# Self-loop products of two node groups in one step, their edge sums in the next; two PSUM banks for the sums and four for the products

## What is computed

```python
h = relu(layernorm(x))
W_rel = einsum('rb,bdf->rdf', w_comp, weight)          # 32 matrices out of 8 bases
agg = segment_sum(h[src] * norm, etype * n_nodes + dst) # edges sorted by dst
node = einsum('rnd,rdf->nf', agg, W_rel) + h_bias + h @ loop_weight
out = x + relu(node)
```

## Time and profile before

| | |
|---|---|
| median of three runs | 1015.2 us |
| the profiled execution | 1015.24 us |
| its span, first to last instruction | 1013.5 us (so 1.7 us lie around it) |
| TensorE busy | 990.3 us, 98% |
| VectorE busy | 955.0 us, 94% |
| ScalarE busy | 884.6 us, 87% |
| GpSimd busy | 723.8 us, 71% |
| granted TensorE clock | 0.999 |

### The profile page before, as it was taken

How to read it: one execution, slowest core, us unless ns; L and a number is a source line. 1 busy time by engine, 2 the same in 40 slices (tenths; PEclk the granted TensorE clock), 3 DMA queues, 4 the chain that set the end, 5 groups by cost and what they waited for, 6 DMA issues and landing times.

```text
span 1013.5 us, 23775 instructions
## 1 busy us (share of the span) xinstructions
PE 990.3 (98%) x4902; PEld 574.4 (57%) x4902; DVE 955.0 (94%) x4366; ACT 884.6 (87%) x3242; POOL 723.8 (71%) x1282
## 2 busy tenths in 40 slices
PE   5899999999999999999999999999999999999996
PEld 2355555555556565656565555555555655555655
DVE  6999999999999999999999999999999999999995
ACT  6898989898888889898989898989898988889884
POOL 6877777777777777777777777777777777777740
PEclk9999999999999999999999999999999999999999
DMA  4556555556556555565565555465655655555544
GB/s 116 145 135 165 149 156 164 156 144 169 143 152 173 140 154 161 152 166 155 143 173 141 154 162 158 138 178 140 168 152 152 166 148 155 159 155 141 156 123 140
DMA packets 178223, 154.47 MB, mean 152 GB/s; under 512 B 17781, under 2 KB 151213, under 8 KB 178077
## 3 DMA queue, kind: packets, MB, share of 16 engines
q1 hardware_dynamic: 157261, 101.40, 35.6%
q0 software_dynamic: 20384, 51.32, 19.7%
q10 hardware_dynamic: 432, 0.22, 0.1%
HBM read 101.31 MB, written 51.56 MB: 151 GB/s over the span
## 4 chain that ended last, share of the span: by engine, by line
PE 93%; DVE 2%; POOL 2%; issue 1%; ACT 1%; DMA 1%; DVEq 0%; ACTq 0%; POOLq 0%
PE y_ps L790 33%; PE y_ps L797 31%; PE win_ps L812 9%; PE win_ps L807 8%; PE hT_ps L876 4%; PE hT_ps L803 4%; PE mix_ps L868 1%; POOL xg L578 1%; DVE sum_a L1019 1%; DVE sum_b L1019 0%; DMA xg<-x,idx 0%; DVE msg L1052 0%; PE y_ps L812 0%; DMA src_all<-src 0%; PE y_ps L807 0%
## 5 line engine op out<-in xcount | busy, mean ns | idle before, releaser
L578 POOL DMA_INDIRECT xg<-x,idx x392 | 382.0, 974 | 73.4 <-issue 34.0
L790 PE MATMUL y_ps<-w_all,hT 128*128 128x512 f32 x784 | 412.3, 608 | 2.9 <-DVE sum_a L1019 2.7
L797 PE MATMUL y_ps<-w_all,hT 128*128 128x512 f32 x784 | 400.3, 592 | 0.0
L523 POOL TENSOR_TENSOR u<-z 128x128 f32<-128x128 f32 x392 | 180.4, 460 | 182.8 <-ACT z L626 178.9
L626 ACT ACTIVATE z<-y_ps,mix 128x128 f32<-128x128 f32 x784 | 244.5, 366 | 44.8 <-PE y_ps L797 37.8
L1019 DVE SCALAR_TENSOR_TENSOR sum_b<-y_ps,mix,sum_b 128x128 f32<-128x128 f32 x784 | 265.8, 339 | 0.0
L797 PEld LDWEIGHTS y_ps<-w_all,hT 128*128 128x128 f32 x784 | 149.1, 190 | 187.9 <-issue 164.0
L790 PEld LDWEIGHTS y_ps<-w_all,hT 128*128 128x128 f32 x784 | 132.3, 189 | 119.1 <-DVE sum_a L1019 60.9
L622 ACT ACTIVATE z<-y_ps,mix 128x128 f32<-128x128 f32 x392 | 140.8, 359 | 63.6 <-issue 44.9
L660 ACT ACTIVATE hw<-xw,shift,nrstd 128x128 f32<-128x128 f32 x391 | 192.6, 494 | 0.4 <-DVE shift L1121 0.4
L1019 DVE SCALAR_TENSOR_TENSOR sum_b<-y_ps,mix,z 128x128 f32<-128x128 f32 x392 | 131.4, 335 | 36.1 <-issue 32.3
(11 more groups left out here) (107 smaller groups left out, 1174.3 us busy)
## 6 DMA issues: line engine op xcount, KB each, us to landing
seg<-msgs SPq DMA_DIRECT2D x391, 104.8 KB
msgs<-msg SPq DMA_DIRECT2D x98, 258.0 KB
xw<-x POOLq DMA_DIRECT2D x97, 256.0 KB
out<-res SPq DMA_DIRECT2D x97, 256.0 KB
xg<-x,idx POOLq DMA_INDIRECT x392
type_bc<-type_rows SPq DMA_DIRECT2D x52, 112.0 KB
w_all<-weight SPq DMA_DIRECT2D x1, 512.0 KB
type_bc<-type_rows SPq DMA_DIRECT2D x4, 80.0 KB
```

The costliest lines, as they stand in the source:

```text
L523: nc.gpsimd.tensor_tensor(u[:, r, :], z[:, r, 0, :], z[:, r, 1, :], ALU.add).then_inc(s_u, 1)
L578: nc.gpsimd.indirect_dma_start(xg[:, q, j, :], None, x, bass.IndirectOffsetOnAxis(ap=idx[:, q, j:j + 1], axis=0)).then_inc(s_gather[q * G ...
L790: nc.tensor.matmul(y_ps[2 * t % 5][:, :, :], hT[:, q, j, :], w_all[:, B // 2:B, :], start=True, stop=True).then_inc(s_y_high, 1)
L797: nc.tensor.matmul(y_ps[(2 * t + 1) % 5][:, :, :], hT[:, q, j, :], w_all[:, 0:B // 2, :], start=True, stop=True).then_inc(s_y, 1)
```

## The change

- The five banks `y_ps` become four, and `win_ps` becomes two banks, used by even and odd node groups. Tile t now has its high product in bank 2t mod 4 and its low product in bank (2t+1) mod 4, so product_high waits for `s_b` of tile t-2 and product_low for `s_a` of tile t-2.
- TensorE does no self-loop products and edge sums in every step. In odd steps g it does the self-loop products of node groups g-7 and g-6 (8 matmuls), in even steps g the edge sums of node groups g-8 and g-7 (16 matmuls), with two node groups open in the two banks in between.
- `pick` moves one step later (VectorE step k+6). `res` of both groups of a pair is made in the even step: the first between slots 1 and 2 behind `pick`, the second behind slot 3, ahead of `hotT`.
- `hwT` and `pick` have three buffers in place of two; a new semaphore `n_self` counts the self-loop products and frees `hwT`.
- There is one more step at the end. The last four node groups use the four `y_ps` banks.

The diff, cut to its core:

```diff
+TRING = 3
+SELF_AT = 7
+PICK_AT = 8
+ROWS_AT = 6
-    STEPS = NGW + SUMS_AT
+    STEPS = NGW + PICK_AT - 1
-        hwT = sb("hwT", [P, HRING, G, P])
+        hwT = sb("hwT", [P, TRING, G, P])
-        pick = sb("pick", [P, HRING, G, HALVES, HALF])
+        pick = sb("pick", [P, TRING, G, HALVES, HALF])
-        y_ps = [psum(f"y_ps{b}", [P, B // 2, F]) for b in range(5)]
-        win_ps = psum("win_ps", [P, G, F])
+        y_ps = [psum(f"y_ps{b}", [P, B // 2, F]) for b in range(4)]
+        win_ps = [psum(f"win_ps{b}", [P, G, F]) for b in range(2)]
...
         def win_of(k):
-            return win_ps if k < NGW - LATE else late_bank(k - (NGW - LATE))
+            return win_ps[k % 2] if k < NGW - LATE else y_ps[k - (NGW - LATE)]
...
             def window_hT(k):
                 act.wait_ge(n_hT, k + 1)
-                if k >= HRING:
-                    act.wait_ge(n_y, k - (HRING - 1))
+                if k >= TRING:
+                    act.wait_ge(n_self, k - (TRING - 1))
...
             def product_high(g, q, j):
                 t = g * G + j
-                if t >= 3:
-                    pe.wait_ge(s_a, 2 * (t - 2))
+                if t >= 2:
+                    pe.wait_ge(s_b, 3 * (t - 1))
...
             def product_low(g, q, j):
                 t = g * G + j
                 if t >= 2:
-                    pe.wait_ge(s_b, 3 * (t - 1))
+                    pe.wait_ge(s_a, 2 * (t - 1))
...
             def window_self(k, j):
...
-                    elif k > 0:
-                        pe.wait_ge(n_res, k)
+                    if k >= NGW - LATE:
+                        pe.wait_ge(s_b, 3 * NG * G)
+                        pe.wait_ge(s_a, 2 * NG * G)
+                    elif k > 1:
+                        pe.wait_ge(n_res, k - 1)
...
-                if node_group(g, SUMS_AT) is not None:
-                    for j in range(G):
-                        window_self(g - SUMS_AT, j)
-                if node_group(g, SUMS_AT) is not None and g != STEPS - 2:
-                    if g == STEPS - 1:
-                        window_sums(NGW - 2)
-                    window_sums(g - SUMS_AT)
+                k = node_group(g, SELF_AT)
+                if k is not None and k % 2 == 0:
+                    for j in range(2 * G):
+                        window_self(k + j // G, j % G)
+                k = node_group(g, PICK_AT)
+                if k is not None and k % 2 == 0:
+                    window_sums(k)
+                    window_sums(k + 1)
...
-                if g == STEPS - 3:
-                    window_results(g - SUMS_AT)
-                if node_group(g, TURN_AT) is not None:
-                    window_rows(g - TURN_AT)
-                if node_group(g, SUMS_AT) is not None and g != STEPS - 3:
-                    window_results(g - SUMS_AT)
+                k = node_group(g, PICK_AT)
+                ready = k is not None and k % 2 == 0
+                late = ready and k >= NGW - LATE
+                if late:
+                    window_results(k)
+                    window_results(k + 1)
+                if node_group(g, ROWS_AT) is not None:
+                    window_rows(g - ROWS_AT)
+                if ready and not late:
+                    window_results(k)
                 tile_slot(g, n, q, 2, False)
...
                 tile_slot(g, n, q, 3, False)
                 stats_of(3)
+                if ready and not late:
+                    window_results(k + 1)
```

More of the change, by code:

```diff
@@ L245, in product @@
             high = base >= B // 2
-            return y_ps[(2 * t + (0 if high else 1)) % 5][:, base % (B // 2), :]
-        def late_bank(i):
-            return y_ps[(2 * NG * G + i) % 5]
+            return y_ps[(2 * t + (0 if high else 1)) % 4][:, base % (B // 2), :]
         def win_of(k):
-            return win_ps if k < NGW - LATE else late_bank(k - (NGW - LATE))
+            return win_ps[k % 2] if k < NGW - LATE else y_ps[k - (NGW - LATE)]
         s_iotas = sem("s_iotas")
@@ L355, in build_layer @@
         n_y = sem("n_y")
+        n_self = sem("n_self")
         n_res = sem("n_res")
@@ L419, in load_node_constants @@
                 sp.dma_start(pick[SEG_P:SEG_P + 1, :, :, :, :].rearrange("p r j c n -> p (r j) (c n)"),
-                             ones[SEG_P:SEG_P + 1, :].unsqueeze(1).to_broadcast([1, HRING * G, P])).then_inc(s_loop, 16)
+                             ones[SEG_P:SEG_P + 1, :].unsqueeze(1).to_broadcast([1, TRING * G, P])).then_inc(s_loop, 16)
                 sp.wait_ge(s_front, 1)
@@ L666, in window_hT @@
                 act.wait_ge(n_hT, k + 1)
-                if k >= HRING:
-                    act.wait_ge(n_y, k - (HRING - 1))
-                nc.scalar.activation(hwT[:, k % HRING, :, :], hT_ps[:, :, :], ACT.Copy).then_inc(n_hT_sb, 1)
+                if k >= TRING:
+                    act.wait_ge(n_self, k - (TRING - 1))
+                nc.scalar.activation(hwT[:, k % TRING, :, :], hT_ps[:, :, :], ACT.Copy).then_inc(n_hT_sb, 1)
             def step(g, n, q):
@@ L774, in count_bins @@
             def count_bins(half):
-                counts = win_ps[0:1, :, :].rearrange("p b f -> p (b f)")
+                counts = win_ps[0][0:1, :, :].rearrange("p b f -> p (b f)")
                 pe.wait_ge(s_first_hot, 1)
@@ L787, in product_high @@
                 t = g * G + j
-                if t >= 3:
-                    pe.wait_ge(s_a, 2 * (t - 2))
-                nc.tensor.matmul(y_ps[2 * t % 5][:, :, :], hT[:, q, j, :], w_all[:, B // 2:B, :],
+                if t >= 2:
+                    pe.wait_ge(s_b, 3 * (t - 1))
+                nc.tensor.matmul(y_ps[2 * t % 4][:, :, :], hT[:, q, j, :], w_all[:, B // 2:B, :],
                                  start=True, stop=True).then_inc(s_y_high, 1)
@@ L795, in product_low @@
                 if t >= 2:
-                    pe.wait_ge(s_b, 3 * (t - 1))
-                nc.tensor.matmul(y_ps[(2 * t + 1) % 5][:, :, :], hT[:, q, j, :], w_all[:, 0:B // 2, :],
+                    pe.wait_ge(s_a, 2 * (t - 1))
+                nc.tensor.matmul(y_ps[(2 * t + 1) % 4][:, :, :], hT[:, q, j, :], w_all[:, 0:B // 2, :],
                                  start=True, stop=True).then_inc(s_y, 1)
@@ L806, in self_loop @@
             def self_loop(bank, v, j):
-                nc.tensor.matmul(bank[:, j, :], hwT[:, v, j, :], w_loop[:, :], start=j == 0, stop=False)
+                return nc.tensor.matmul(bank[:, j, :], hwT[:, v, j, :], w_loop[:, :], start=j == 0, stop=False)
             def edge_sums(bank, v, q, windows):
@@ L822, in window_self @@
                     pe.wait_ge(n_hT_sb, k + 1)
[L823 to L829, removed]
-                    elif k > 0:
-                        pe.wait_ge(n_res, k)
+                    if k >= NGW - LATE:
[3 more added lines that the diff above has]
+                        pe.wait_ge(n_res, k - 1)
                 if j < windows_of(k):
-                    self_loop(win_of(k), k % HRING, j)
+                    mm = self_loop(win_of(k), k % TRING, j)
+                    if j == windows_of(k) - 1:
+                        mm.then_inc(n_self, 1)
             def window_sums(k):
                 pe.wait_ge(n_pick, k + 1)
-                edge_sums(win_of(k), k % HRING, k % SRING, windows_of(k)).then_inc(n_y, 1)
+                edge_sums(win_of(k), k % TRING, k % SRING, windows_of(k)).then_inc(n_y, 1)
             def step(g, n, q):
@@ L905, in _ @@
                     for j in range(G):
-                        self_loop(win_ps, 0, j)
-                    edge_sums(win_ps, 0, 0, G).then_inc(f_y, 1)
+                        self_loop(win_ps[0], 0, j)
+                    edge_sums(win_ps[0], 0, 0, G).then_inc(f_y, 1)
         @block.vector
@@ L963, in row_table @@
                 dve.wait_ge(s_hist, 1)
-                nc.vector.tensor_copy(hist[:, :], win_ps[0:1, :, :].rearrange("p b f -> p (b f)")[:, 0:BINS]).then_inc(s_meta, 1)
+                nc.vector.tensor_copy(hist[:, :], win_ps[0][0:1, :, :].rearrange("p b f -> p (b f)")[:, 0:BINS]).then_inc(s_meta, 1)
                 dve.wait_ge(s_meta, 1)
@@ L1132, in window_rows @@
             def window_rows(k):
-                if k >= HRING:
-                    dve.wait_ge(n_y, k - (HRING - 1))
+                if k >= TRING:
+                    dve.wait_ge(n_y, k - (TRING - 1))
                 dve.wait_ge(n_rel, k + 1)
-                one_hot_rows(k % HRING, k % NRING, windows_of(k)).then_inc(n_pick, 1)
+                one_hot_rows(k % TRING, k % NRING, windows_of(k)).then_inc(n_pick, 1)
             def results(bank, r, q, windows):
@@ L1248, in again @@
                 hold(dve, passed["dve"])
-                results(win_ps, 0, 0, G).then_inc(f_res, 1)
+                results(win_ps[0], 0, 0, G).then_inc(f_res, 1)
             with dve.If(compact > 0):
```

## The result

| | before | after |
|---|---|---|
| median | 1015.55 us (4 runs) | 1153.61 us (4 runs) |
| ratio | | 1.136, 95% interval 1.134 to 1.137 |
| span of the profiled execution | 1013.5 us | 1151.4 us |
| TensorE busy | 990.3 us, 98% | 1025.7 us, 89% |
| VectorE busy | 955.0 us, 94% | 981.1 us, 85% |

The forecast was 1142 us with a range of 1115 to 1170. The kernel became 138 us slower, 11.6 us more than forecast.

What follows compares the result with a forecast made beforehand. TensorE, 98% of the span, was taken to bound the kernel. With bank waits making a longer loop, span 1013.5 + 123.4 + 1.2 + 1.9 = 1140, and 1.7 around it, gave 1142 us; range 1115 to 1170.

Steps and rivals of the forecast that it cites:

- The bank releases: TensorE's low products: with four banks, `sum_a` frees the bank 0.59 us late for low m0, 1.10 for low m1.
- Slot 3 hangs on T: VectorE starts slot 3 at T+2.51 whatever TensorE does, because it waits for ScalarE's `z`, which follows T.
- T: Start of the edge transposes on TensorE in a step, from which the prediction counts its times.
- The second res in the loop at 0.60: VectorE, between slots 3 and 0: the second `res` makes `sum_a` of m3 0.60 us later in every other loop.
- The saving of 0.33 us per round trip: TensorE entering (0.14) and leaving (0.19) half-width sums once per two steps: about 46 x 0.33 = 15 us saved.
- the tail: End of the run: last edge step +1.2 us, sums of groups 94 and 95 behind the last transposes +1.9.
- Restart of 0.10: TensorE product behind a bank wait: the wait costs 0.10 us extra, bounds 0 and 0.19.
- the fourth rival: TensorE's clock falls because it idles; one loop in ten at 1.2 GHz adds 90 us, giving 1232; 2%.
- GpSimd and seg, taken at nothing: Later `res` delays SyncE's `seg` loads, holding GpSimd half a microsecond; covered by a microsecond, so no cost taken.
- the faster rival: Product banks are free in time and the regrouping's saving stands: 1002 us; 5%.
- The sum over steps 7 to 97: 45 pairs of loops, 11.27 and 11.53 us, 22.80 per pair in place of 20.07: 1026.0 us.
- The start: First steps, up to the loop of step 6: change of 0 us, give or take 2.

Runs made afterwards that it cites:

- the control: Kernel before, five banks and no regrouping, with the mix product moved into the transposes' bank behind messages(3) and VectorE's mix behind slot 3: 1022.3 us, ratio 1.0065.

## Why the prediction was right

- **The bank releases.** Right as read. The two waits, the instruction that ends them and the loop through ScalarE and VectorE are in the trace, to within 0.1 us; the four banks alone cost 125.6 us. One sign was mis-sized: I had said some 137 us of TensorE idle, 3.1 per pair, and the trace has 0.49 + 0.83 + 0.49 + 0.23 = 2.04 per pair, 103.5 in all. I counted from the time at which the product was due. The record of the product ahead reaches 0.16 us beyond that (1.02 against 0.86), and the restart of 0.10 falls behind the start.
- **Slot 3 hangs on T.** Right: T+2.51 in both loops shown; only with the block moved ahead of it did it come later, at T+2.79. This is what made the sum possible; had VectorE followed TensorE's delay in another way, the rows of before would not have told the new step.
- **The second res in the loop at 0.60.** Right: 27.5 us for 45.
- **The saving of 0.33 us per round trip.** The sum holds: 13.0 us against the control with five banks, where the forecast terms give 46 x 0.33 less 2 for the tail, 13. In the changed kernel it lies inside the loop and so is taken off it: 15.0 us between the two kernels with four banks. The measured parts, 125.6 for the banks, 15.0 off for the regrouping and 27.5 for the second `res`, lead from the kernel before to the changed one step by step and make its 138.
- **Restart of 0.10.** Right: a product behind a wait is followed after 0.96 (604.70 to 605.66), others after 0.86. By the 166 ns that the Trainium skill ("TensorE: Matmul & The Clock Gate", Single matmul latency) has for an isolated bf16 matmul the run would be 6 us longer, as an estimate. The loops, 11.56 and 11.27 against 11.53 and 11.27 with the row, decide for the row here. That the run is 6.4 us longer over steps 7 to 97 has other reasons, named below.
- **The clock.** TensorE idled in every loop and the granted clock was 1.00 of the 2.4 GHz level from 72 to 1115 us and up to the last matmul, so the fourth rival did not come. The run with five banks and later stores shows such a fall, on an idle time longer than any in the loops. In the tail of its profiled execution TensorE waited 2.51 us for `pick`, and the 28 matmuls behind that took 2.96 us in place of the 1.75 shown above:

```profile
1001.78 2.96 PE L813 MATMUL y_ps<-seg,pick 105*64 105x128 f32 x28 [2.51 <-DVE pick L1128]
```

The granted clock was 1.00 up to 1002 us and 0.52 from 1002 to 1005, near the 1.2 GHz level. That execution took 1011.03 us, the other four 1008.7 to 1009.3.
- **GpSimd and seg, taken at nothing.** The cost was right, the size of the wait was not. I had half a microsecond and some covered waits; in steps 6 to 97 there were 36 of 1.0 us in the mean. In the loop shown above SyncE issues the loads, and GpSimd takes them, like this:

```profile
601.60 1.89 SPq L442 DMA_DIRECT2D seg<-msgs  x4
```

```profile
606.39 0.20 POOL L548 TENSOR_TENSOR rel<-seg,half_off 104x8 f32<-104x8 f32 x1 [0.96 <-DMA seg<-msgs]
```

`res` ends 0.6 us before T and not 0.8; the first load is issued 1.2 us behind that, where my sum has 0.5 to 1; and so `rel` starts at T+5.39 and not at T+4.5 to T+5. The waits cost nothing in these steps because the bank waits covered them. Without these they cost 36 us, so in the faster rival the 1002 us could not have come either.
- **Mis-sized terms, 11 us together.** The sum over steps 7 to 97 came out 6.4 us short. I had listed what stands behind slot 3 and left out the nine order checks at its end, which the loop then carried: 3.8 us measured; some 1.4 us are the 0.03 us per pair by which the loops are longer; the last 1.2 us, in a few single loops, I have not taken apart. The start cost 2.9 and not 0, since the bank waits were there before any node work. The tail was 2 us longer than its term, by two waits for `pick` behind the last seg loads; with later stores they are gone, and the tail is 3.3 us longer than before, where I had 3.1.

## What to carry to other kernels

Where an engine is busy without a gap, the order behind it may still depend on slack that no busy share shows: write down for each buffer when it is wanted and when it is released, and move the want by what the change moves it. If the release is late, look for what the releasing instruction itself waits on; if that leads back to the stalled engine, the new step is the length of that loop, and everything that stands in it costs its full time, on an engine with 15% to spare too. What is taken out of the loop comes back only until the next wait ends last: 15 us of 33 here. When one thing has been taken away that everyone waited for, look again at the waits that it covered: one constant in the store order was worth 1.7 us beside the bank waits, all of it in the tail, and 36 us without them.

## What the runs showed that I had not expected

A 512-wide product that follows a mix product (32 columns) takes 0.94 us of the chain and not 0.86. In the kernel before, the edge transposes stand there and cost 0.47 where the node transposes cost 0.44; and in the control, where no mix product stands ahead of them, they cost 0.44 as well. So the mix product costs 0.14 us and 0.03 more ahead of these transposes, or 0.08 more ahead of a 512-wide product. Over 91 steps 0.05 us each are 4.6 of the control's 6.8 us.
